# A decoder kernel's expert layer: inverse deviations by square root and Newton step in place of a power

## What is computed

```
def _layernorm(x, axis=-1, eps=1e-05):
    m = jnp.mean(x, axis=axis, keepdims=True)
    v = jnp.var(x, axis=axis, keepdims=True)
    return (x - m) / jnp.sqrt(v + eps)

tokens = x_flat[index].reshape(E, expert_capacity, hidden)
inter = jax.nn.relu(jnp.einsum('ech,eih->eci', tokens, first_linear))
out = jnp.einsum('eci,ehi->ech', inter, second_linear)
out = out * vals[:, :, None]
final = jnp.zeros((n_tokens, hidden), x.dtype).at[index].add(out.reshape(-1, hidden))

x = _layernorm(x + _L0_ffn_ref(x, ...), axis=-1)
```

## Time and profile before

| | before |
|---|---|
| timed runs | 1020.33 us median of 3 (1018.7 to 1022.15) |
| the profiled execution | 1013.04 us, its span 1010.9 us |
| granted TensorE clock | 0.995 |
| PE | 980.9 us busy (97%) |
| DVE | 823.5 us (81%) |
| ACT | 724.2 us (72%) |
| POOL | 587.9 us (58%) |
| chain that ended last | PE 79%, ACT 6%, DVE 6%, issue 4%, POOL 2% of the span |

### The profile page before, as it was taken

The page is one execution under the profiler, slowest core; times in us unless marked ns, Lnnn a source line. Parts: engine busy times, 40 slices in busy tenths (PEclk is TensorE's granted clock), DMA queues, the critical chain, the costliest instruction groups (busy, mean ns, idle before and its releaser), DMA issues.

```text
span 1010.9 us, 21647 instructions
## 1 busy us (share of the span) xinstructions
PE 980.9 (97%) x7018; PEld 928.6 (92%) x7018; DVE 823.5 (81%) x2087; ACT 724.2 (72%) x1857; POOL 587.9 (58%) x1069
## 2 busy tenths in 40 slices
PE   8999999999999999999999999999999999999993
PEld 6789999999999999999999999999999999889993
DVE  6887878888888888887888788878888887767774
ACT  6686877777787768786878677877777766547761
POOL 4743465665566656665575637565665464536786
PEclk9999999999999999999999999999999999999997
DMA  7663031112211131104110402031112213555542
GB/s 249 193 143 109 16 110 47 51 46 88 69 52 46 59 98 52 47 18 140 51 46 2 135 29 58 33 110 47 51 46 91 98 31 124 193 173 163 170 149 88
DMA packets 63030, 88.97 MB, mean 88 GB/s; under 512 B 15540, under 2 KB 44008, under 8 KB 62920
## 3 DMA queue, kind: packets, MB, share of 16 engines
q1 hardware_dynamic: 56968, 71.10, 22.8%
q0 software_dynamic: 5952, 16.50, 4.9%
HBM read 49.31 MB, written 38.26 MB: 87 GB/s over the span
## 4 chain that ended last, share of the span: by engine, by line
PE 79%; ACT 6%; DVE 6%; issue 4%; POOL 2%; DMA 1%; POOLq 0%; SPq 0%; DVEq 0%; ACTq 0%
PE ps L629 21%; PE ps L631 21%; PE ps L630 21%; PE ps L658 7%; PE ps L737 3%; DVE nmx L1838 2%; PE ps L673 1%; PE ps L675 1%; PE ps L775 1%; ACT hp L1094 1%; PE ps L768 1%; ACT prob L1251 1%; POOL out L2327 1%; PE ps L761 1%; DMA cxs<-in_ctxt 1%
## 5 line engine op out<-in xcount | busy, mean ns | idle before, releaser
L2212 POOL TENSOR_SCALAR prob<-prob,rinv 128x333 f32<-128x333 f32 x256 | 143.5, 572 | 234.5 <-DVE rinv L1847 234.0
L1246 ACT ACTIVATE oT_hi<-ps 128x256 fp32r<-128x256 f32 x126 | 48.4, 384 | 150.5 <-PE ps L675 150.5
L629 PE MATMUL ps<-kv_lo,w_hi 128*128 128x256 f32 (+1 forms) x512 | 154.9, 303 | 1.1 <-DVE kv_lo L1398 1.1
L631 PE MATMUL ps<-kv_hi,w_hi 128*128 128x256 f32 (+1 forms) x512 | 152.9, 299 | 0.0
L630 PE MATMUL ps<-kv_hi,w_lo 128*128 128x256 f32 (+1 forms) x512 | 152.5, 298 | 0.0
L1251 ACT ACTIVATE prob<-ps,nmx 128x333 f32<-128x333 f32 x256 | 134.8, 537 | 7.7 <-DVE nmx L1838 7.7
L1398 DVE TENSOR_TENSOR pT_lo<-ps,pT_hi 128x512 fp32r<-128x512 f32 x254 | 130.8, 549 | 0.9 <-ACT pT_hi L1263 0.3
L1838 DVE TENSOR_REDUCE nmx<-ps 128x2 f32<-128x666 f32 x128 | 108.4, 847 | 8.4 <-PE ps L631 7.0
L658 PE MATMUL ps<-ident,prob 128*128 128x128 f32 (+1 forms) x768 | 105.9, 273 | 1.8 <-POOL prob L2212 1.0
L629 PEld LDWEIGHTS ps<-kv_lo,w_hi 128*128 128x128 f32 x512 | 96.9, 189 | 1.7 <-issue 1.5
L631 PEld LDWEIGHTS ps<-kv_hi,w_hi 128*128 128x128 f32 x512 | 96.8, 189 | 0.0
(11 more groups left out here) (330 smaller groups left out, 3319.3 us busy)
## 6 DMA issues: line engine op xcount, KB each, us to landing
wraw<-in_W SPq DMA_DIRECT2D x14, 512.0 KB, 5.2
vcd_hi<-vst_hi SPq DMA_DIRECT2D x10, 512.0 KB, 2.7
vcd_lo<-vst_lo SPq DMA_DIRECT2D x10, 512.0 KB, 3.7
v_hi<-vcd_hi SPq DMA_DIRECT2D x32, 154.0 KB
v_lo<-vcd_hi SPq DMA_DIRECT2D x32, 154.0 KB
slots<-initr SPq DMA_DIRECT2D x8, 522.0 KB, 9.9
xs<-in_x SPq DMA_DIRECT2D x16, 256.0 KB, 4.3
xts<-in_xT SPq DMA_DIRECT2D x15, 256.0 KB, 4.0
```

The source lines that it names most:

```text
L629: pe.matmul(dst, hi1, lo2, start=first, stop=False, skip_group_check=True)
L631: return pe.matmul(dst, hi1, hi2, start=False, stop=last, skip_group_check=True)
L2212: pool.tensor_scalar(prob[:, h % 2, t, 0:KEYS], prob[:, h % 2, t, 0:KEYS], rinv[:, h % 2, t:t + 1], 1.0, ALU.mult, ALU.mult).then_inc(norm ...
```

## The change

The factor `f_rs` of the experts is made by a square root on ACT (`deviation`, into `f_sd`), then on DVE by a reciprocal and one Newton step (`inverse`), four instructions, each waiting for the one before. POOL's `power` is gone. One activation with a square root is put at the end of ACT's part of the last batch. ACT's square root of expert `e - 1` stands between the third and the fourth tile of `relu(e)`; in the tail four of them follow the relu tiles. `block_moments` moves behind `weights(1)`, `block_norm` behind the `shift` of the loop's first pass. In the last batch DVE makes only row 0 of `c_vv` and POOL's power (L2185) takes only this row and waits for two results fewer. POOL's tail is one gather and eight stores without powers between. SP's and PE's lists are the same.

```diff
@@ ACT, ending
                 block_relu()
                 xparts(0)
+                act.activation(warm[:], warm[:], ACT.Sqrt)
@@ ACT, experts
+            def deviation(part, e, tiles):
+
+                act.wait_ge(fstat_set, 3 * part + 3)
+                act.activation(f_sd[:, e, tiles], f_vv[:, e, tiles], ACT.Sqrt).then_inc(fsd_set, 1)
...
-                need(act, fnm_set, part + 1)
+                need(act, fnm_set, 5 * (part + 1))
...
-                relu(e)
+                relu(e, range(0, 3))
+                deviation(e - 1, e - 1, slice(0, ST))
+                relu(e, range(3, 4))
...
             last_relu(1, (0, 1))
+            deviation(E - 2, E - 2, slice(0, 3))
+            deviation(E - 1, E - 2, slice(3, 4))
             scale(E - 2, T_ORDER[0:3], E - 2)
             scale(E - 2, T_ORDER[3:4], E - 1)
             last_relu(1, (2, 3))
+            deviation(E, E - 1, slice(0, 2))
+            deviation(E + 1, E - 1, slice(2, 4))
@@ DVE, residual_stats
                 dve.tensor_scalar(c_vv[:, 0, :], c_mv[:, :, 1], 1.0, EPS, ALU.mult, ALU.add).then_inc(cstat_set, 1)
+                if at(b, B):
+                    return
@@ DVE, experts
+            def inverse(part, e, tiles, steps):
+
+                o = (slice(None), e, tiles)
+                dve.wait_ge(fsd_set, part + 1)
+                dve.reciprocal(f_r0[o], f_sd[o]).then_inc(fnm_set, 1)
+                dve.wait_ge(fnm_set, steps + 1)
+                dve.scalar_tensor_tensor(out=f_cr[o], in0=f_r0[o], scalar=-0.5, in1=f_r0[o], op0=ALU.mult,
+                                         op1=ALU.mult).then_inc(fnm_set, 1)
+                dve.wait_ge(fnm_set, steps + 2)
+                dve.tensor_tensor(f_cr[o], f_cr[o], f_vv[o], ALU.mult).then_inc(fnm_set, 1)
+                dve.wait_ge(fnm_set, steps + 3)
+                dve.scalar_tensor_tensor(out=f_rs[o], in0=f_cr[o], scalar=1.5, in1=f_r0[o], op0=ALU.add,
+                                         op1=ALU.mult).then_inc(fnm_set, 1)
+                dve.wait_ge(fnm_set, steps + 4)
+
             def shift(part, e, tiles):
 
-                dve.wait_ge(frs_set, part + 1)
+                inverse(part, e, tiles, 5 * part)
...
             relu(0)
-            block_moments()
             part1(1, 1)
             dve.wait_ge(sc_done, 64 * B)
             part2(1, 1)
-            block_norm()
             xparts(1)
             weights(1, 1, 16)
+            block_moments()
             sums(0, 0)
...
                 shift(e - 1, e - 1, slice(0, ST))
+                if e == 1:
+                    block_norm()
                 xparts(e + 1)
...
-                dve.wait_ge(frs_set, part + 1)
+                inverse(part, e, slice(tiles[0], tiles[-1] + 1), 5 * E + 4 * (part - E))
@@ POOL, ending
-                pool.wait_ge(cstat_set, 7 * B)
-                pool.tensor_tensor(c_rs[:].rearrange("p c t -> p (c t)"), c_vv[:].rearrange("p c t -> p (c t)"), powm[:],
-                                   ALU.pow).then_inc(crs_set, 1)
+                pool.wait_ge(cstat_set, 7 * B - 2)
+                pool.tensor_tensor(c_rs[:, 0, :], c_vv[:, 0, :], powm[:, 0:NT], ALU.pow).then_inc(crs_set, 1)
@@ POOL, experts
             for e in range(1, E - 1):
-                power(e - 1, e - 1, slice(0, ST))
                 gather(e)
                 finished(e - 1, range(ST))
-            power(E - 2, E - 2, slice(0, 3))
-            power(E - 1, E - 2, slice(3, 4))
             gather(E - 1)
-            finished(E - 2, (0, 1, 2), T_ORDER)
-            power(E, E - 1, slice(0, 2))
-            finished(E - 2, (3,), T_ORDER)
-            power(E + 1, E - 1, slice(2, 4))
+            finished(E - 2, range(ST), T_ORDER)
             finished(E - 1, range(ST))
```

More of the change, by code:

```diff
@@ L280, in build @@
         f_vv = s2("f_vv", [P, E, ST])
+        f_sd = s2("f_sd", [P, E, ST])
+        f_r0 = s2("f_r0", [P, E, ST])
+        f_cr = s2("f_cr", [P, E, ST])
         f_rs = s2("f_rs", [P, E, ST])
@@ L341, in build @@
         lrs_set, z_set, bs_ld = sem("lrs_set"), sem("z_set"), [sem("bs_ld0"), sem("bs_ld1")]
-        fstat_set, frs_set, fnm_set, fo_set = sem("fstat_set"), sem("frs_set"), sem("fnm_set"), sem("fo_set")
+        fstat_set, fsd_set, fnm_set, fo_set = sem("fstat_set"), sem("fsd_set"), sem("fnm_set"), sem("fo_set")
         bs0_ld, z_st, own_st, last_st = part_ld[0:4]
@@ L1321, in _, with relu @@
             ending()
-            def relu(e):
-                for i in range(I // P):
+            def relu(e, tiles=range(I // P)):
+                for i in tiles:
                     need(act, h_mm, 4 * stage(e) + i + 1)
@@ L2298, in _ @@
             ending()
[L2301 to L2305, removed]
             def gather(e):
```

## The result

The changed kernel took 1031.25 us (1030.12 to 1031.7), the kernel before 1020.33: ratio 1.0091 [1.0073, 1.011], 10.9 us slower. Forecast were +5.75 and 1026.1, at most 1029.5. The direction was right, the size was nearly twice the forecast. The profiled execution took 1030.31 us, 1028.6 of it span. Up to 880 us it is 1.5 us later than the profiled execution before, in the attention part, which the change doesn't touch; so 1.5 is taken off where times are compared.

A forecast was written before the change was run, and what follows sets the result against it. TensorE, busy 97% of the span, was taken as the bound. Stall with fallen clock +7.4, last batch -0.45 and tail -1.2 gave +5.75: 1018.8 us like the profiled execution, 1026.1 against the median; range 1018.5 to 1029.5.

The forecast's parts named there:

- Last batch: POOL's shorter power, waiting for one DVE row instead of three, brings all that follows forward: -0.45 us.
- The table: One load of the square root's table fits ACT's idle time before expert 0's first relu: no cost, otherwise 1.5 us.
- rival 4: ACT reloads tables between square root and relu, two loads in each of seven experts: +12, 1032 us; chance 0.05.
- Start of the loop: PE's weight load no longer waits for `xs_lo` behind the last batch's moments and norm: -0.35 us.
- Newton steps: Four more dependent DVE operations cost +0.8 us per expert on DVE, hidden by 1.4 us of slack.
- SP held: SP waits for the moved norm, delaying expert 0's stores and expert 1's gathers; PE stalls before expert 2's outer product: +5.7 us.
- the clock: After PE's 5.5 us gap the clock falls to half; outer product 2 loses 2.3 us: +7.4 instead of +5.7.
- Tail: Without POOL's powers the last gathers and indirect stores come earlier: -1.2 us, bounds -0.5 and -2.2.
- The sum: Stall with fallen clock, last batch and tail together: +5.75 us, chance 0.45.
- after this the loop catches its old order: Behind the stall, a gather needs about 10.7 us from sum to sum against the expert loop's 12.2 us pitch.

The follow-up runs named there:

- e7_one_row: Kernel before with only the last batch's power on one row of variances instead of two, two DVE steps left out: 1013.39 against 1014.06 us, ratio 0.9995.
- e2_old_order: Changed kernel with the last batch's moments and norm back in their old places in DVE's order: 1012.54 us against 1013.85 for the kernel before, ratio 0.9985.
- e5_after_again: Changed kernel, unchanged, on a third chip: 1018.88 us against 1014.06 for the kernel before, ratio 1.0048.
- e3: Changed kernel with SP's output store of the last batch behind the stores of expert 0's sums: 1011.91 us against 1013.85 for the kernel before, ratio 0.9978.
- e6: Changed kernel with ACT's square root behind the fourth relu instead of ahead of it: 1020.31 us against 1014.06 for the kernel before, ratio 1.0059.
- e12: Same kernel as e3 (changed kernel, last batch's output store later), run again: 1011.93 us with the kernel before at 1014.23, ratio 0.9979.
- e1: Kernel before, unchanged, profiled once more: 1013.66 us beside 1013.85 for the kernel before on the same chip.
- e10_before_third: Kernel before, unchanged, in its own run on the chip of e9_after_third: 1021.83 us.
- e9_after_third: Changed kernel, unchanged, a third time on another chip: 1032.17 us against 1022.25 for the kernel before, ratio 1.0094.

## Why the prediction was right and wrong

- **Last batch, -0.45.** Held in the first trace; e7_one_row can't tell it from nothing.
- **The table, 0.** Held. One load more, in the gap where it was put, and none in the loop, which ends rival 4:

```profile
896.14 1.28 ACT L1316 ACT_TABLE_LOAD   x1
897.43 0.20 ACT L1316 ACTIVATE warm<-warm 128x4 f32<-128x4 f32 x1
899.85 0.60 ACT L1332 ACTIVATE h_hi<-ps 128x512 fp32r<-128x512 f32 x1 [2.21 <-issue]
```

- **Start of the loop, -0.35.** Held: in the trace before, the inner product of expert 1 began 0.14 us behind the last end of the outer product; in the first trace after, it begins ahead of that end, like the other inner products.
- **Newton steps, 0.8 on DVE, hidden.** Held: five steps 0.2 apart, and e2_old_order, which has them all, is 1.3 us faster than before (forecast for it -0.45 - 1.2 = -1.65).
- **SP held, +5.7, and the clock, +1.7.** Held in place and, within 1 us, in size. In e5_after_again the outer product of expert 2 began at 933.27 after 5.19 us of idleness (forecast 933.26 and 5.5) and the inner product behind it at 940.30; there the clock was at half for 3.4 us, in the first trace for 6.8, in which it began at 941.4. For the slow clock 2.3 us had been put on that outer product of 5.9; it took 7.2 in e5_after_again and 8.6 in the first trace, 1.3 and 2.7 more. From expert 1 to 5 the changed kernel loses 55.4 - 48.6 = 6.8 us, the move alone 7.2, against 7.4.
- **Tail, -1.2.** Where no counts are late, it agrees loosely. The five traces with the changed tail (e2, e3, e5, e6, e12) have 41.9 to 43.3 in the table, the three of before with their tail (before, e1, e7) 42.7 to 43.9: 0.8 less in the mean, and the two overlap. The gather that stood at [2.08 <-issue] in the earlier trace rows still does, with 2.13, so leaving that delay in was right. Where counts are late, the tail failed, see below.
- **The sum, +5.75.** Where no counts are late it is +4.8 [3.5, 6.1]. Held there.
- **Three steps failed where the result was measured.** The first is the one that carried the sum from the profiled execution to the median: "1018.8 for an execution like the profiled one, 1026.1 against the median". It took the 7.3 us between the two for spread on top of the same course of events. They were most likely of another chip, on which the expert loop runs otherwise: the timed runs of the kernel before take 1012.6 to 1015.9 us on three chips and 1018.5 to 1028.7 on two and in the first result, with none between, and the trace before has the mark of the first kind (see the last section). On a chip of the profile's kind the changed kernel takes 1018.9, as forecast, on the others 1031 to 1032.
- The second is "after this the loop catches its old order". On the chips of the profile's kind the pitch is 12.1 to 12.2. On the others, in both traces of the changed kernel, ACT gets TensorE's counts mostly 2 to 4 us late in expert after expert, DVE's second sum of each expert waits for it (3.2 us each in experts 3 to 5 of the first trace), and the stall isn't made up but added to.
- The third is "Tail: -1.2". On such chips the three traces with the changed tail and all scatters have 47.5, 48.8 and 50.3 us behind expert 5, where e10_before_third, the only trace of before, has 45.4: +2.1 to +5.0.
- The extra is 10.9 - 4.8 = 6.1 us on the first chip, 5.1 on that of e9_after_third. Since the kernel before is slower there too (52.9 instead of 48.6 from expert 1 to 5), the difference between the kernels from 1 to 5 is 8.4 and 7.3 us against 6.8 elsewhere. So, as far as one trace of before can tell, more of the extra lies behind expert 5 than in the loop. No rival had it; that rival 4's 1032 comes near the measured time is chance, for its table loads aren't there.
- **Sums.** 933.26 + 5.73 is 938.99 and not 939.05, and the upper bounds named (6.5 and 3, less 0.45 and 1.2) give 1028.2 and not 1029.5. Neither bears on the outcome.

What stays open: why some chips deliver these counts late, and why the changed kernel is hit 5 us more than the one before. That its late stores put each scatter onto the end of an outer product (956.50 beside 956.44 above) is no explanation by itself: in the trace before, scatters start at 945.85, 958.01 and 970.16 beside outer products that end at 946.27, 958.40 and 970.59, and in e10_before_third one stands beside a count that is on time. Nor is it known which kind of chip was used where only a median is given.

## What to carry over

When a norm or any late result is moved, look first at the queue that stores it: here the moments and the norm, 1.2 and 0.7 us of DVE's time, could move at no cost, and the store of it, ahead of two others in SP's order, cost some 7 us; putting the store behind them turned the change into a gain of 1.9 and 2.3 us on two chips without late counts, and into no difference that can be told on one with them. When the profiled execution and the median differ by more than the runs do among themselves (7.3 us against 3.5 here), the trace may be of another course of events than the one that is timed: forecast against each, and widen the range by what the difference could do to the change.

## What the runs showed of the hardware

- The same program takes 1014 us on three chips and 1021 to 1022 on two others; the first result is like those two. On the latter the matmuls' counts reach other engines up to 5.8 us after the matmul's end, mostly beside POOL's gathers or scatters, though the matmuls themselves go on at their pitch. Not every scatter does it. Such traces also hold fewer records of landed transfers: 5,606 in the first trace after and 5,650 in e10_before_third, 6,912 in the trace before; all five have 5,583 to 5,650, and the others with all their scatters 6,910 to 6,920. A wait that the profile puts down to a store can be such a count.
- POOL's drain ends the trace; it takes 5.8 to 7.3 us that begin beside its last four scatters. With 24 scatters fewer it took 11.9 and 12.7 us. Why is open.
- After a gap of 5.2 us the granted clock was at half for 3.4 us in one trace (e5_after_again) and for 6.8 in another (the first one after); after one of 2.6 us (e10_before_third) for 3.4.
